# One attention-and-mixture network of four layers on one core: weights split inside the first pass, loads by need, a new order of steps

## The chip, the cores and the metric

The kernel runs on one core of a Trainium2 chip. The metric is the device time of one execution in microseconds (us). TensorE (PE) multiplies, VectorE (DVE), ScalarE (ACT) and GpSimd (POOL) do the rest, and SyncE (SP) issues all DMA transfers from its own in-order queue. Each engine runs its instructions in order and waits on semaphores for the others. SBUF is the on-chip memory of 128 partitions, PSUM the accumulator memory that PE writes.

## The reference, cut

The batch has 16 elements of 256 tokens x 256 features. Each element goes through four layers, and each layer is an attention over a context and a feed-forward part, both added with a tanh gate:

```python
x = x + tanh(g_xattn[0]) * L0_xattn(layernorm(x), ctx)   # 32 half heads of 8, differential attention
x = x + tanh(g_ffn[0])   * L0_ffn(layernorm(x))          # three cycles of a gated coupling net
x = x + tanh(g_xattn[1]) * L1_xattn(ctx, layernorm(x))   # 8 heads of 64, 512 keys, masked
x = x + tanh(g_ffn[1])   * L1_ffn(layernorm(x))          # mixture: 2 shared + 8 routed experts, silu
x = x + tanh(g_xattn[2]) * L2_xattn(layernorm(x), ctx)   # 16 heads of 16
x = x + tanh(g_ffn[2])   * L2_ffn(layernorm(x))          # inner attention, then 8 experts, gelu, top 2
x = x + tanh(g_xattn[3]) * L3_xattn(layernorm(x), ctx)   # one head
x = x + tanh(g_ffn[3])   * L3_ffn(layernorm(x))          # relu, rounded to 8-bit floats
```

L2_ffn is the second mixture. For each of its eight experts it needs `h1 = gelu(m @ w1 + b1)` and `h1 @ w2`, with w1 of 256 x 512 and w2 of 512 x 256.

## The kernel before

**Passes and steps.** Two batch elements are worked on at a time (slots 0 and 1); eight passes make up the batch. The work of one element is cut into named steps with a number: l0.max.0.3 is the fourth row maximum of layer 0 for element 0. One list, SCHEDULE, holds all 4288 steps; the string ORDER writes out by hand, one character per step, from which of 18 lists the next step comes (9 lists for each slot: the main chain, four for context work, one for values and back transposes, one for the mean path of f0, one for init, one for the first steps of layer 0). Every engine walks the same SCHEDULE and issues its own part of each step. So the order of work on PE, ACT, DVE and POOL is this one order, and steps of pass 1 stand mixed among the last steps of pass 0.

**Names.** ctxT, l0.ln, l0.xT, l0.k, l0.v, l0.ks, l0.q, l0.qs, l0.max, l0.shift, l0.exp, l0.pv, l0.out make up the first attention. l0.max is PE (L561) and one DVE reduction of 128 x 1024 (L1146). l0.shift turns the maxima (DVE L1160 to L1165, PE L502). f0.h1, f0.h2 (L512), f0.h3 (L713) and f0.t (L717) are the chain of the coupling net, each of which needs the activation that ACT makes of the one before. f2.up (PE L765) and f2.down (PE L775) are the second mixture: up is followed by a gelu on ACT (L884) and by a cast and a subtraction on DVE (L1458, L1459), down by an addition to x on DVE (L1116). PSUM has three work banks for all these products: the n-th product waits until the one three before it was read.

**The split weights.** The second mixture multiplies in the fast reduced-precision form of fp32, three products for one: each weight w is kept as hi (w rounded) and lo (w - hi). Before the schedule starts, eight experts are split: SP loads the raw expert into va (L1556), ACT copies it rounded into ksp (L870), DVE subtracts into qsp (L1349), and SP stores both to the DRAM tensor split (L1554, L1555), two experts in flight. ACT then waits until all stores are done before its first step of the schedule. In each of the eight passes SP loads hi and lo of each expert back from split, into va_hi and stream_lo, a ring of two experts.

**The launch.** SP loads all resident weights in one transfer (L1540), then stage (selection matrices, L1541), then context (cx) and x of both slots (L1546, L1547). DVE waits for the resident weights and does a chain of small setup operations (L1301 to L1342), among them four casts of the selection matrices (L1330); ACT does tanh and exp for it (L862, L864). PE waits for s_setup 1 (after the cast of w2q, L1332). ksp lies in the upper half of k1; l0.ks writes it, and l0.max and l0.exp read it.

Of the kernel before, what the change touches and what calls it, by code (L numbers as in the profile page):

```python
# [10 lines left out]
P = 128  # L11
# [34 lines left out]
    ("ident", 128), ("g_x", 4), ("g_f", 4), ("lam", 32), ("subln", 16),  # L46
# [14 lines left out]
RESIDENT_COLS = sum(n for _, n in RESIDENT)  # L61
LATE_COLS = sum(n for _, n in LATE)
# [6 lines left out]
class HeadPlan:  # L69
# [122 lines left out]
LISTS = 9  # L192
# [4 lines left out]
def lists_of(s):  # L197

    def aside(step):
        if step[0] in FIRST:  # L200
            return len(ASIDE)
        kinds = [n for n, whats in enumerate(ASIDE) if step[0].split(".")[-1] in whats and step[0] != "l3.pv"]
        return kinds[0] if kinds else None

    main, context = slot_steps(s), context_steps(s)
    every = context[0] + main
    return [[x for x in steps if aside(x) is None] for steps in (main, *context)] \
        + [[x for x in every if aside(x) == n] for n in range(len(ASIDE) + 1)]
# [3 lines left out]
    "A718A18HG111A8H8AH88A8H88HHH888888HH8H8888888HHH0H0HHH50505H50HH0HHH50509559055E0E59E99EE99E0E9095E509EE9E500E9E95950E95"  # L212
    "E2590EEE09029090696076G09F06009B90F0F009F09B0920B0000929B099000990009900009000909090095905095995950959095099099595795909"
    "E090E93E9EEE909E0900EE0E099G030900C9C90990990990390909090990099009909309809900900C90C00090000090909905905909509595090959"
    "055995990E9E09E9E9E90E907EE00E09009080G90009000099999009990990059095095095099550095595H9E90E9E009E4900E9E974EE01E091GD91"
    "9D9A91098990988089809A890980808988098090898A0909A89089080897800HH90G0H90H0H9088091090HH0909HH000H99550A05050H5H0H50H50H5"
    "H055095H05H0H5050H9H9550H9959E95E709E9E9E9E9E9E09E0E9E90E9E29E0E99E6E6E60690020909090090F09F09BF0F90909009B90900229909B9"
    "00090G090900000B0990095095590959909059590595990995959090E9EE99E3E79E9E9EE00E39000933900C90909900909090090099099099099G09"
    "9009009C0900990C90C00909000900990090905509990509950590505957959890E9E90E9E9E9E09E0E00E00090G9090000900090099990909905905"
    "09590599050590595949597940E9E09E900E09E9E190E8EH0E19H91G919890D89D9A98A89808A909A0890908H890980H98098088089H80H98909078H"  # L220
    "09H010H90900G90H8080H9A0H90009980009H95500505H050505H905H095505H0H505H050H50H9H55H9959E9E9E9E90E92E9E0E9E09E9E9E09E9E9E9"
    "0E6EE606690020099900090F0F09F09F90B9B07090990009992G90B0020900900900090090B50909959095995059999059909550959599E090E9EE9E"
    "90E9E97EE0E090090093003909099C99G09909900990099090900390909903099C9090C09C9900990000000090099009550990509590505095595990"
    "E9E90EE99E9E900EE0E07090G09090000900900009999090H099505909509509509959095549579890E9E90E0E908E909E94E0E1E019D9191G998098"
    "D9A0898A9A890A89H0890898098H08H909809800H9098H0980H90HH900899000908808987001908H090H9HH00950H0H5H0H55900G5050H5H5500H59H"
    "09H505HA09550099505E9592E59E9E90E9E9E9EE9E0E909E9E9E9E90E0E6E60G966002090900900900990FF79FF900B0090909B0999B902002009000"
    "900900990090505909959959B09095995995990059595907E0E99EE90E09E9E9EE0E003909039303G090999090090909009909C0909090990990099C"
    "090909C90000909000C00009099509905909590590995050595959890E9E09E9E9E9E90E070EE009000900900900009G999900999089090950959059"
    "095905050955995E90E9E07H9E0904EE0994EE0GD1E019D9911998A09889089A80A89HA8908H89980H890890H89H0909808H9H098H09HH09H08H0900"
    "909078G0A098080910908090H9H00905H50H05095050H5050H59H0550H505050H5909H50595995E97E9E9E09E9E9E09E0E9E9E09E9E9E069E960E2E6"  # L230
    "0E600090B0009009B009090F0G9F09F0029B9BF902900090909090920909009909900505050995905995905599999099959599E90E097E9E09EEE993"
    "EE0GE00093093090C90999009900990099009909090099009903099C90090C9090C009090009009900990990505909509505905059595980E990E90E"
    "9E97E9H0E9E00E0E0G0909090009000009099890990095905909590590950950995549959E09E9E90HE0907E09E94EE10E0G9D19D11999809899A089"
    "08909098089980889080898098908980890890A870900AAH909H0H1H9HHH090HGH0H990H0A998009088000H50H5H0590505H05H050H5055H0505H050"
    "955H090H595995E097E9E9E92E9E9E09E0E9E9E9E90E9E096E960EBE6EG609200029990009009FF9F00F909090B090990990290B9000900009000090"
    "900509505959900599955900559597909999B9099E90E9E0E990EEE990EEE0930933093C0090099900990909099099090900990090G909C90H9900C9"
    "090C009900090090900990990550909590590505909559H59E09E900E9E9E9E79E00E0E0900G90090009090000099990909950909590590959059095"
    "0595959E089E0E0990E940E7E9948E0E1D0E1G9D991A9910989088980A8980889A8A98090H98089089H80H9089H0H98H090898H0909H0090098090GH"
    "088097A01H090909H00905H050H5H0H505095050H590H55H5H909H500H5099505905E95E925E9E9E9E9E90E9EE0E9009E9E9E9E90EE6E60006290609"
    "990700900F9F09F0B9F909009009B90909209B020090090000090G9B900059990559090595950995090999959595990E90E09EE9E9E0E909EEGE0093"  # L240
    "090C907039099909900990099009900909090003309C0099099099C990C0090000000909099050995095095990590950599557990E9EH090E9E9E9E0"
    "9E00E0000E00900990090000G999H909909950095059095099509590955495909E9E9800E9E7908E09E49E0E10E190199GD19D9A809899089A890A89"
    "8A908H9H0H809089H90H980H0898H09H908908089009G0A9089090H07899H8019089900088000H50HH50505H05H05H5005H05505H95009H595H0950H"
    "0995E5E959E9E9E9E9E9E009EE9E0E990E9E90E69E2606E6E00920029900909F0090GF0F909F90B0B90970990299009B00B090000009009909900595"
    "00595050590959059995995999099099E9E9EE907E90E09E090EE0E09090C093099990099099099G00909309090909099003399C090CC90909000009"
    "9000000909905099590950950950959509595909E09E9E09E9E0900E79E00E00E00900909009G09009999090990590959095909509509505957959E9"
    "0E9E90E9E090E09EEE09094G9990D9990990909090090909099090490900900D900909090990099900909909"
# [10 lines left out]
SCHEDULE = in_order()  # L258

# [24 lines left out]
def build(nc, x_in, ctx_in, mask_in, resident_in, stage_in, moe1_in, moe2_in, out):  # L284
    with ExitStack() as ctx:
# [75 lines left out]
        k1, ksp, pt_spread = [], [], []  # L361
# [38 lines left out]

        s_res = sem("s_res")
        s_raw = [sem("s_raw0"), sem("s_raw1")]
        s_split_hi = sem("s_split_hi")
        s_split_lo = sem("s_split_lo")
        s_kept = [sem("s_kept0"), sem("s_kept1")]
# [55 lines left out]
        def split_buffers(e):  # L461

            i = e % 2
            return (va[i][:, 0:MOE2_COLS], ksp[i][:, :, :].rearrange("p a t -> p (a t)"), qsp[i][:, :, :].rearrange("p a t -> p (a t)"))
# [14 lines left out]
        def pass_of(s):  # L479

            return s // SLOTS
# [3 lines left out]
        def _(pe):  # L485
# [40 lines left out]
            def spread_attention(plan, what, s, u):  # L526
# [12 lines left out]
                elif what in ("ks", "qs"):  # L539

                    w = take(st + "." + what, s, u)
                    pe.wait_ge(*after("s_lo", st + "." + what[0], s))
                    sel = {32: {"q": sel8q, "k": sel8k}, 64: {"q": sel16q, "k": sel16k}}[plan.rows][what[0]]
# [191 lines left out]
            def ffn_2(what, s, e):  # L735
# [20 lines left out]
                elif what == "up":  # L756

                    pe.wait_ge(S[f"s_moe2_{e % RING2}"], 32 * (pass_of(s) * MOE2 // RING2 + e // RING2 + 1))
# [100 lines left out]
        def _(act):  # L859
            act.wait_ge(s_res, 16)  # L860
            for j, (name, a) in enumerate((("g_x", 0), ("g_f", 4))):
# [879 lines left out]
```

## Time and profile before

| | |
|---|---|
| median of 3 runs | 5006.4 us (5000.1 to 5006.8) |
| profiled execution | 5007.3 us |
| its span, first to last instruction | 5005.5 us |
| PE busy | 4456.6 us, 89% |
| DVE busy | 2957.9 us, 59% |
| ACT busy | 1929.4 us, 39% |
| mean granted TensorE clock | 0.948 of full |
| HBM read / written | 219.1 / 21.0 MB |

The span is one profiled execution. "Idle before" is time in which an engine waited for the instruction named behind the arrow. A window row gives each engine's busy time in one stretch. PEclk 1.00 is the 2.4 GHz level of TensorE's clock, 0.50 the 1.2 GHz level, and values between are means over a stretch.

### The profile page before, as it was taken

What the parts mean: (1) busy time and instruction counts of PE and PEld (TensorE: products, weight loads), DVE (VectorE), ACT (ScalarE), POOL (GpSimd) and SP (SyncE); (2) the same over time, 40 slices, a digit from 0 to 9 for tenths busy, and PEclk for the clock granted to TensorE, in tenths of its full rate; (3) what the DMA queues carried; (4) which work ended last, traced back from release to release, by engine and by line L of the source; (5) the groups of instructions that cost most, each with busy time, mean ns of one, the idle gap of its engine ahead of it and who ended that gap; (6) DMA issues with size and microseconds to landing.
All of it is one profiled execution on the core that took longest, in us unless ns stands there. A gap on an engine that the chain in (4) does not pass through costs nothing.

```text
span 5005.5 us, 74404 instructions
## 1 busy us (share of the span) xinstructions
PE 4456.6 (89%) x29184; PEld 3371.1 (67%) x29184; DVE 2957.9 (59%) x7749; ACT 1929.4 (39%) x3134; POOL 109.2 (2%) x196
## 2 busy tenths in 40 slices
PE   2798898989989899898998989989899988989889
PEld 1467685766756677576775758667596675856658
DVE  4556666566655566556666465655665556655555
ACT  2332535434353342433434343442434425343242
POOL 0000000000000000000000000000000000000000
PEclk9899999999989999999999989999899999999999
DMA  7001020011200111001210003001030010200012
GB/s 289 1 13 36 26 110 26 13 36 60 77 26 16 34 77 60 26 16 33 85 68 9 30 20 127 35 1 49 18 118 26 13 36 26 110 26 13 28 38 102
DMA packets 53785, 244.88 MB, mean 49 GB/s; under 512 B 5056, under 2 KB 21440, under 8 KB 31680
## 3 DMA queue, kind: packets, MB, share of 16 engines
q1 hardware_dynamic: 53440, 240.11, 13.0%
q8 instruction: 237, 3.88, 0.3%
q14 instruction: 108, 0.88, 0.1%
HBM read 219.12 MB, written 20.97 MB: 48 GB/s over the span
## 4 chain that ended last, share of the span: by engine, by line
PE 61%; DVE 9%; ACT 3%; issue 2%; POOL 0%; DVEq 0%; ACTq 0%
PE w L512 13%; PE w L522 8%; PE o L657 7%; PE w L765 7%; PE w L775 6%; PE w L502 3%; PE o L650 3%; PE w L578 3%; DVE mx L1146 2%; PE w L628 2%; PE w L613 2%; PE w L561 2%; PE w L669 1%; PE w L631 1%; DVE x L1116 1%
## 5 line engine op out<-in xcount | busy, mean ns | idle before, releaser
L1146 DVE TENSOR_REDUCE mx<-w 128x4 f32<-128x1024 f32 x512 | 606.8, 1221 | 154.9 <-PE w L561 128.2
L933 ACT ACTIVATE pt_spread<-w 128x1024 f32<-128x1024 f32 x512 | 518.8, 1024 | 294.6 <-PE w L578 277.9
L657 PE MATMUL o<-pt_spread,va 128*32 128x256 f32 x4096 | 533.8, 395 | 18.9 <-ACT pt_spread L933 17.5
L884 ACT ACTIVATE oth<-w,res 128x256 f32<-128x256 f32 x656 | 277.3, 471 | 614.1 <-PE w L765 435.1
L512 PE MATMUL w<-xnT,stream 128*128 128x256 f32 x1792 | 421.8, 385 | 8.0 <-DVE tmp L1110 3.8
L512 PEld LDWEIGHTS w<-xnT,stream 128*128 128x128 f32 x1792 | 340.4, 192 | 58.8 <-DVE tmp L1110 4.4
L765 PE MATMUL w<-qodd,va_hi 128*128 128x256 f32 x2048 | 350.1, 285 | 5.6 <-DVE x L1116 4.3
L657 PEld LDWEIGHTS o<-pt_spread,va 128*32 128x32 f32 x4096 | 203.6, 111 | 192.8 <-issue 48.2
L1116 DVE SCALAR_TENSOR_TENSOR x<-w,gate,x 128x256 f32<-128x256 f32 x512 | 224.2, 479 | 174.3 <-PE w L775 143.6
L561 PE MATMUL w<-ksp,qsp 32*128 32x256 f32 (+1 forms) x2048 | 255.5, 362 | 58.6 <-DVE mx L1146 30.4
L765 PEld LDWEIGHTS w<-qodd,va_hi 128*128 128x128 f32 x2048 | 285.7, 189 | 17.0 <-DVE x L1116 7.7
L561 PEld LDWEIGHTS w<-ksp,qsp 32*128 32x128 f32 (+1 forms) x2048 | 164.6, 217 | 153.1 <-DVE mx L1146 60.9
L578 PEld LDWEIGHTS w<-qsp,ksp 32*128 32x128 f32 (+1 forms) x2048 | 148.0, 189 | 173.8 <-issue 129.3
L578 PE MATMUL w<-qsp,ksp 32*128 32x256 f32 (+1 forms) x2048 | 241.0, 331 | 20.1 <-DVE qsp L1165 13.3
L876 ACT ACTIVATE oth<-o 128x256 f32<-128x256 f32 (+1 forms) x384 | 146.8, 382 | 265.8 <-PE o L650 159.3
L512 PE MATMUL w<-xnT,res 128*128 128x256 f32 x768 | 226.1, 442 | 22.5 <-ACT xnT L876 14.8
L650 PE MATMUL o<-pt,va 128*65 128x256 f32 x1024 | 238.1, 379 | 0.1
L1410 DVE TENSOR_REDUCE mx<-w 128x2 f32<-128x1024 f32 x128 | 154.1, 1226 | 114.0 <-PE w L615 113.9
L522 PE MATMUL w<-stream,oth 128*128 128x256 f32 x640 | 173.8, 396 | 37.3 <-DVE oth L1427 33.6
L765 PE MATMUL w<-qodd,stream_lo 128*128 128x256 f32 x1024 | 205.2, 282 | 0.0
L933 ACT ACTIVATE pt<-w 128x1024 f32<-128x1024 f32 x128 | 131.1, 1024 | 188.3 <-PE w L631 188.2
L512 PEld LDWEIGHTS w<-xnT,res 128*128 128x128 f32 x768 | 160.9, 220 | 61.7 <-issue 27.8
(269 smaller groups left out, 8222.2 us busy)
## 6 DMA issues: line engine op xcount, KB each, us to landing
stream_lo<-split SPq DMA_DIRECT2D x64, 1024.0 KB, 4.8
va_hi<-split SPq DMA_DIRECT2D x64, 1024.0 KB, 6.9
stream<-in_moe_dram SPq DMA_DIRECT2D x80, 384.0 KB, 3.1
stream<-in_resident_dram SPq DMA_DIRECT2D x8, 2048.0 KB, 7.4
va<-in_moe_dram SPq DMA_DIRECT2D x8, 1024.0 KB, 10.4
split<-ksp SPq DMA_DIRECT2D x8, 1024.0 KB, 5.6
split<-qsp SPq DMA_DIRECT2D x8, 1024.0 KB, 7.9
stream<-in_resident_dram SPq DMA_DIRECT2D x8, 1024.0 KB, 4.7
```

Of the source, the lines that this page charges most:

```text
L512: mm = pe.matmul(w[:, col0 + j * T:col0 + j * T + T], weight[:, k, (m0 + j) * P:(m0 + j + 1) * P], act[:, k, :], start=(k == 0), stop=(k = ...
L522: mm = pe.matmul(w[:, o:o + n], act[:, k, tt * P:(tt + 1) * P], weight[:, k, :], start=(k == 0), stop=(k == kc - 1))
L561: mm = pe.matmul(w[:, a * 512 + tt * T:a * 512 + (tt + 1) * T], qsp[s][b:b + plan.rows, c, tt * P:(tt + 1) * P], ksp[s][b:b + plan.rows, c ...
L578: mm = pe.matmul(w[:, a * 512 + kt * T:a * 512 + (kt + 1) * T], ksp[s][b:b + plan.rows, c, kt * P:(kt + 1) * P], qsp[s][b:b + plan.rows, c ...
L650: mm = pe.matmul(o[0:L1_DIM + 1, 0:T], by_heads1(s)[:, kt, u, :], p[:, kt * T:(kt + 1) * T], start=(kt == 0), stop=(kt == KT - 1))
L657: mm = pe.matmul(o[g:g + 32, 0:T], by_heads(plan, s)[:, kt, plan.v_of(h), :], p[:, a * 512 + kt * T:a * 512 + (kt + 1) * T], start=(kt == ...
L765: mm = pe.matmul(w[:, j * T:(j + 1) * T], wt[:, k, j * P:(j + 1) * P], a[:, k, :], start=(n == 0), stop=(n == len(parts) - 1))
L775: mm = pe.matmul(w[:, tt * D:(tt + 1) * D], a[:, k, tt * P:(tt + 1) * P], wt[:, k, :], start=(n == 0), stop=(n == len(parts) - 1))
L884: h = act.activation(dst[:, c, :], w[:, c * T:(c + 1) * T], func, bias=bias[:, c:c + 1], **more)
L933: act.activation(exp_buffer(plan.name + ".exp", s, u), w[:, :], ACT.Exp, scale=scale).then_inc(S["s_P"], 1)
L1116: h = dve.scalar_tensor_tensor(x[s][:, tt, :], w[:, tt * stride:tt * stride + D], gate_ap(tt), x[s][:, tt, :], ALU.mult, ALU.add)
L1146: dve.tensor_reduce(mx[s][:, :, 2 * u:2 * u + 2].rearrange("p t a -> p a t"), w[:, :].rearrange("p (a t k) -> p a t k", a=2, t=TT), AX_X, ...
```

## The change

- The loop that splits the weights ahead of the schedule is gone. Eight steps f2.split take its place in SCHEDULE, in a tenth list of slot 0, all in pass 0. In each, ACT writes hi straight into va_hi and DVE writes lo straight into stream_lo, where up and down read them. raw is a new name for the place of ksp.
- In pass 0 SP loads raw experts in place of hi and lo, and stores hi and lo to split for the passes after. PE's up waits for s_wlo in pass 0. l0.ks of pass 1 waits for split 6 or 7, l0.init of pass 1 and SP's load of f3_w1 for the stores.
- The resident load is cut in two. The first 2178 columns (of 10171) hold what the first steps need, ones8 and ones16 among them; stage is cut into selections (1024 columns) and the rest. SP issues first slice, selections, context and x, rest of resident, rest of stage.
- Engines wait for the rest, and DVE and ACT do the setup, where the first step comes that is not in EARLY. In the new order that is l0.shift.0.0, the 43rd step, behind 21 steps l0.max.
- ORDER is a new string of 4296 steps. All steps of before are in it, in other places.

```diff
-    ("ident", 128), ("g_x", 4), ("g_f", 4), ("lam", 32), ("subln", 16),
+    ("ident", 128), ("ones8", 1), ("ones16", 1), ("g_x", 4), ("g_f", 4), ("lam", 32), ("subln", 16),
...
+FIRST_COLS = 4 * 512 + 128 + 2
+SELECT_COLS = 4 * 256
...
-LISTS = 9
+LISTS = 10
...
+        + [[("f2.split", s, e) for e in range(MOE2)] if s == 0 else []]
...
+EARLY = ("ctxT", "l0.k", "l0.v", "l0.ks", "l0.ln", "l0.xT", "l0.q", "l0.qs", "l0.max", "l0.init", "l1.cln")
+FIRST_LATE = next(x for x in SCHEDULE if x[0] not in EARLY)
...
+            raw.append(nc.alloc_sbuf_tensor_at(f"raw{s}", [P, MOE2_COLS], F32, offset=nc.sbuf_base - half))
...
-            pe.wait_ge(s_res, 16)
-            pe.wait_ge(s_setup, 1)
+            pe.wait_ge(s_first, 16)
             for step, s, u in SCHEDULE:
+                if (step, s, u) == FIRST_LATE:
+                    pe.wait_ge(s_res, 16)
+                    pe.wait_ge(s_setup, 3)
...
-            for e in range(MOE2):
-                raw, hi, _ = split_buffers(e)
-                act.wait_ge(s_raw[e % 2], 16 * (e // 2 + 1))
-                if e >= 2:
-                    act.wait_ge(s_kept[e % 2], 32 * (e // 2))
-                act.activation(hi, raw, ACT.Copy).then_inc(s_split_hi, 1)
...
+                    if plan is L0 and pass_of(s) == 1:
+                        act.wait_ge(*after("s_wlo", "f2.split", 0, MOE2 - 2 + s % SLOTS))
...
+                elif step == "f2.split":
+                    if u < 2:
+                        act.wait_ge(*after("s_pv", "f2.pv", u, F2.units - 1))
+                    else:
+                        for other in range(SLOTS):
+                            full(act, "f2.down", other, u - RING2)
+                        act.wait_ge(s_kept[u % 2], 32 * (u // 2))
+                    act.wait_ge(s_raw[u % 2], 16 * (u // 2 + 1))
+                    act.activation(expert2(u)[0], raw2(u), ACT.Copy).then_inc(S["s_whi"], 1)
...
+                elif step == "f2.split":
+                    dve.wait_ge(*after("s_whi", step, s, u))
+                    if u < RING2:
+                        for other in range(SLOTS):
+                            full(dve, "f1.down", other, MOE1 - 1)
+                    hi, lo = expert2(u)
+                    dve.tensor_tensor(lo, raw2(u), hi.bitcast(F32), ALU.subtract).then_inc(S["s_wlo"], 1)
...
-            sp.dma_start(res[:, :], resident_in[:, 0:RESIDENT_COLS]).then_inc(s_res, 16)
-            sp.dma_start(stream[:, :], stage_in).then_inc(s_stage, 16)
+            sp.dma_start(res[:, 0:FIRST_COLS], resident_in[:, 0:FIRST_COLS]).then_inc(s_first, 16)
+            sp.dma_start(stream[:, 0:SELECT_COLS], stage_in[:, 0:SELECT_COLS]).then_inc(s_sel, 16)
...
+            sp.dma_start(res[:, FIRST_COLS:], resident_in[:, FIRST_COLS:RESIDENT_COLS]).then_inc(s_res, 16)
+            sp.dma_start(stream[:, SELECT_COLS:], stage_in[:, SELECT_COLS:]).then_inc(s_stage, 16)
...
+                if p == 0:
+
+                    for e in range(RING2):
+                        full(sp, "f2.exp", both[e], F2.units - 1)
+                        sp.dma_start(raw2(e), moe2_in[e]).then_inc(s_raw[e % 2], 16)
+                    for e in range(MOE2):
+                        hi, lo = expert2(e)
+                        sp.wait_ge(*after("s_wlo", "f2.split", 0, e))
+                        if e + RING2 < MOE2:
+                            sp.dma_start(raw2(e + RING2), moe2_in[e + RING2]).then_inc(s_raw[e % 2], 16)
+                        sp.dma_start(split[e, 0], hi.bitcast(F32)).then_inc(s_kept[e % 2], 16)
+                        sp.dma_start(split[e, 1], lo.bitcast(F32)).then_inc(s_kept[e % 2], 16)
```

## Rows read from the trace of the kernel before

**Rows 1.** The page, busy time and share of the span of each engine.
```profile
PE 4456.6 (89%) x29184; PEld 3371.1 (67%) x29184; DVE 2957.9 (59%) x7749; ACT 1929.4 (39%) x3134; POOL 109.2 (2%) x196
```
**Rows 2.** Timeline: start, duration, engine, line, operation, count, idle before and releaser.
```profile
15.36 0.30 ACT L862 ACTIVATE tg<-res 128x4 f32<-128x4 f32 x2 [13.35 <-DMA res<-in_resident_dram]
15.42 0.17 DVE L1301 MEMSET onesf<- 128x128 f32 x1 [15.42 <-DMA res<-in_resident_dram]
...
24.39 1.94 PE L502 MATMUL w<-res,cx 128*128 128x128 f32 x8 [24.39 <-DVE w2q L1332]
...
25.99 0.15 DVE L1342 TENSOR_SCALAR nlam<-nlam 128x1 f32<-128x1 f32 x1
...
89.92 1.08 ACT L876 ACTIVATE ctxT<-w 128x512 f32<-128x512 f32 x2 [8.69 <-DMA split<-qsp]
...
90.58 5.48 PE L512 MATMUL w<-ctxT,res 128*128 128x256 f32 x16 [64.24 <-ACT ctxT L876]
...
135.88 0.20 DVE L1160 CAST hib<-mx 128x64 bf16<-128x64 f32 x1
```
**Rows 3.** Windows at the start: busy of each engine, PEclk, DMA share, GB/s.
```profile
24.36:83.47 59.11, 1.94 (x8) 1.57 (x8) 19.57 (x13) 15.37 (x9) 0.00 (x0) 1.00 0.93 375
...
109.90:135.90 26.00, 16.40 (x104) 10.91 (x104) 24.06 (x22) 2.64 (x3) 0.00 (x0) 0.59 0.00 1
```
**Rows 4.** Groups by line, 25 to 84 us: busy, mean ns, idle before.
```profile
L1349 DVE TENSOR_TENSOR qsp<-va,ksp 128x2048 fp32r<-128x2048 f32 x8 | 18.3, 2292 | 39.1 <-ACT ksp L870 39.1
L870 ACT ACTIVATE ksp<-va 128x2048 fp32r<-128x2048 f32 x8 | 15.3, 1908 | 40.4 <-DMA va<-in_moe_dram 40.4
```
**Rows 5.** Groups by line on DVE, 109 to 136 us.
```profile
L1146 DVE TENSOR_REDUCE mx<-w 128x4 f32<-128x1024 f32 x21 | 24.0, 1218 | 2.8 <-PE w L561 2.8
```
**Rows 6.** Windows between the ends of the second mixture, longest, shortest and sum.
```profile
1934.00:2551.00 617.00, 561.98 (x3668) 424.07 (x3668) 371.19 (x966) 238.45 (x390) 13.34 (x25) 0.94 0.12 43
...
4359.00:4958.00 599.00, 539.30 (x3471) 408.04 (x3470) 339.76 (x915) 226.13 (x374) 13.48 (x24) 0.94 0.12 43
sum 4234.00, PE 3867.27 PEld 2925.43 DVE 2534.92 ACT 1663.85 POOL 94.72; mean PE 552.47 PEld 417.92 DVE 362.13 ACT 237.69 POOL 13.53
```
**Rows 7.** Windows of the launch's first 10 us; the last number is GB/s.
```profile
0.00:5.00 5.00, 0.00 (x0) 0.00 (x0) 0.00 (x0) 1.28 (x1) 0.20 (x4) 1.00 0.77 260
5.00:10.00 5.00, 0.00 (x0) 0.00 (x0) 0.00 (x0) 0.00 (x0) 0.00 (x0) 1.00 0.92 399
```
**Rows 8.** DMA issues, 0 to 120 us: KB each, median us from issue to landing.
```profile
res<-in_resident_dram SPq DMA_DIRECT2D x1, 5085.5 KB, 14.6
stream<-in_stage_dram SPq DMA_DIRECT2D x1, 2048.0 KB, 19.0
```
**Rows 9.** Windows: pass 0's second mixture, the stretch after it, the last pass's mixture.
```profile
620.00:722.00 102.00, 100.28 (x833) 94.91 (x832) 68.62 (x123) 30.99 (x67) 0.69 (x2) 1.00 0.36 135
724.00:758.00 34.00, 31.10 (x191) 25.18 (x189) 21.59 (x61) 11.81 (x22) 0.67 (x2) 1.00 0.00 1
4870.00:4958.00 88.00, 87.89 (x731) 87.25 (x729) 49.59 (x106) 23.52 (x57) 0.00 (x0) 1.00 0.41 156
```
**Rows 10.** Groups by line on DVE, 4870 to 4960 us.
```profile
L1459 DVE TENSOR_TENSOR oth_lo<-oth,ob_hi 128x512 fp32r<-128x512 f32 x29 | 20.1, 693 | 1.0
L1116 DVE SCALAR_TENSOR_TENSOR x<-w,gate,x 128x256 f32<-128x256 f32 x32 | 14.0, 479 | 20.9 <-PE w L775 20.9
L1458 DVE CAST ob_hi<-oth 128x512 fp32r<-128x512 f32 x29 | 12.4, 427 | 16.5 <-ACT oth L884 16.5
```
**Rows 11.** Groups by line on PE, whole span: h2, h3 and t of f0.
```profile
L512 PE MATMUL w<-oth,res 128*128 128x256 f32 x192 | 57.0, 423 | 24.5 <-ACT oth L884 23.0 <-ACT gsm L971 1.5
L713 PE MATMUL w<-oth,res 128*64 128x256 f32 x96 | 32.6, 425 | 15.8 <-ACT oth L884 15.8
...
L717 PE MATMUL w<-res,oth 64*128 64x1 f32 x192 | 31.0, 263 | 14.3 <-ACT oth L986 13.9
```

More of the change, by code:

```diff
@@ L248 @@
+    "A57AA5FAF0AFA0F0AF0AF0AFFF0A0AAAA0AHAA0AA0A04A0A0A0A0EA0A00A0A4A0A00A00EA0A00A0A0AA0A0A0A0A0AA0A"
 )
@@ L360, in build @@
         qsp, qz = shared("qsp", [P, 8, T], F32R, "qz", [P, L1_HEADS, T])
-        k1, ksp, pt_spread = [], [], []
+        k1, ksp, pt_spread, raw = [], [], [], []
         for s in range(SLOTS):
@@ L459, in expert2, with raw2 @@
             return va_hi[e % RING2][:, :], stream_lo[:, cols]
-        def split_buffers(e):
-            i = e % 2
-            return (va[i][:, 0:MOE2_COLS], ksp[i][:, :, :].rearrange("p a t -> p (a t)"), qsp[i][:, :, :].rearrange("p a t -> p (a t)"))
+        def raw2(e):
+            return raw[e % 2][:, :]
         def first_and_second(w):
@@ L859, in _ @@
         def _(act):
-            act.wait_ge(s_res, 16)
-            for j, (name, a) in enumerate((("g_x", 0), ("g_f", 4))):
-                act.activation(tg[:, a:a + 4], W_[name], ACT.Tanh).then_inc(s_setup_act, 1)
-            act.wait_ge(s_setup, 2)
-            act.activation(nlam[:, 2:4], nlam[:, 0:2], ACT.Exp).then_inc(s_setup_act, 1)
-            for e in range(MOE2):
-                raw, hi, _ = split_buffers(e)
-                act.wait_ge(s_raw[e % 2], 16 * (e // 2 + 1))
-                if e >= 2:
-                    act.wait_ge(s_kept[e % 2], 32 * (e // 2))
-                act.activation(hi, raw, ACT.Copy).then_inc(s_split_hi, 1)
-            for n in range(2):
-                act.wait_ge(s_kept[n], 32 * (MOE2 // 2))
-            act.wait_ge(s_setup, 3)
+            act.wait_ge(s_first, 16)
             def evac(out_ap, in_ap, sig):
@@ L946, in _ @@
                 stage, what = step.split(".") if "." in step else (step, "")
+                if (step, s, u) == FIRST_LATE:
+                    act.wait_ge(s_res, 16)
+                    for j, (name, a) in enumerate((("g_x", 0), ("g_f", 4))):
+                        act.activation(tg[:, a:a + 4], W_[name], ACT.Tanh).then_inc(s_setup_act, 1)
+                    act.wait_ge(s_setup, 2)
+                    act.activation(nlam[:, 2:4], nlam[:, 0:2], ACT.Exp).then_inc(s_setup_act, 1)
+                    act.wait_ge(s_setup, 3)
                 if step == "ctxT":
@@ L1314, in once @@
                 dve.wait_ge(setup_chain, count[0])
-            lam = W_["lam"].rearrange("p (n d) -> p n d", n=4)
-            for j in range(2):
-                once(dve.tensor_tensor(tmp[:, 8 * j:8 * j + 8], lam[:, 2 * j, :], lam[:, 2 * j + 1, :], ALU.mult))
-                once(dve.tensor_reduce(nlam[:, j:j + 1], tmp[:, 8 * j:8 * j + 8], AX_X, ALU.add))
-            once(dve.memset(first_row[0:1, :], 1.0))
-            once(dve.tensor_scalar(subw[:, :], W_["subln"], 1.0 - LAMBDA_INIT, None, ALU.mult))
@@ L1338, in _ @@
-            dve.wait_ge(s_setup, 2)
-            dve.wait_ge(s_setup_act, 3)
-            once(dve.tensor_tensor(nlam[:, 0:1], nlam[:, 3:4], nlam[:, 2:3], ALU.subtract))
-            dve.tensor_scalar(nlam[:, 0:1], nlam[:, 0:1], LAMBDA_INIT, None, ALU.subtract).then_inc(s_setup, 1)
-            dve.wait_ge(s_setup, 3)
-            for e in range(MOE2):
-                raw, hi, lo = split_buffers(e)
-                dve.wait_ge(s_split_hi, e + 1)
-                if e >= 2:
-                    dve.wait_ge(s_kept[e % 2], 32 * (e // 2))
-                dve.tensor_tensor(lo, raw, hi.bitcast(F32), ALU.subtract).then_inc(s_split_lo, 1)
+                h = dve.tensor_copy(t[:, :, :], sg[:, 256 * j:256 * j + 256].rearrange("p (a b) -> p a b", a=2))
@@ L1596, in _ @@
                     context_and_first(p + 1)
-                for e in range(MOE2):
+                if p == 0:
[9 more added lines that the diff above has]
+                        sp.dma_start(split[e, 1], lo.bitcast(F32)).then_inc(s_kept[e % 2], 16)
+                    for n in range(2):
+                        sp.wait_ge(s_kept[n], 32 * (MOE2 // 2))
+                for e in range(MOE2 if p else 0):
                     n = e % RING2
```

166 lines of the change are left out of this document (86 added, 80 removed), and 4 rows, old and new, of tables (RESIDENT, SIGNALS).

## The prediction

> **What bounds the kernel now.** I read the busy shares first: PE works 89% of the span, DVE 59%, ACT 39% [rows 1]. TensorE bounds the kernel, but only as a mean over stages with different limits, so I cut the span into stretches.
>
> The first stretch is not bound by PE at all. Until 15.4 us everything waits for one load of all resident weights; VectorE then works through its setup, and PE starts its first transposes at 24.39 us [rows 2]. After those eight transposes PE does nothing until 90.58 us [rows 2]. The window 24.36 to 83.47 us shows why: PE 1.94 us busy, DVE 19.57, ACT 15.37, DMA engines 93% busy [rows 3]. It is the split of the second mixture's weights, a loop over eight experts with two buffers. Its own arithmetic is 8 x 2.292 us on DVE and 8 x 1.908 us on ACT [rows 4], and the rest of the time it waits for 24 MB to pass through the DMA queue. The scheduled steps of ACT may not begin before it is over: the first ctxT eviction stands at 89.92 us [rows 2].
>
> Then comes a stretch that DVE bounds: from 109.90 to 135.90 us DVE is 24.06 us busy of 26 [rows 3], 21 reductions of 1.218 us [rows 5], and the first shift's DVE work begins at 135.88 us [rows 2]. From there on eight passes follow. I cut them where the last second-mixture matmul of each pass ends: seven intervals, 4234 us together, mean 604.9, shortest 599, longest 617, PE 552 us busy in each on average [rows 6]. Each interval has its own hand-searched order of the same work, so their spread tells what an order is worth.
>
> **The launch.** The order that the diff gives has the same 21 reductions ahead of the first shift as before, and the same number of steps ahead of the first reduction, so I move this whole piece along as a block, hung on the start of l0.k on PE (90.58 us before).
>
> When can it start? The first slice is 2178 columns, 1.12 MB; the selections 0.52 MB; each context or x tile 0.26 MB. The first step, ctxT of slot 1, needs the slice and cx1, which stands 2.43 MB into the queue. The queue moved 260 GB/s in its first 5 us and 399 GB/s in the next 5 [rows 7], so 1.30 MB by 5 us and 2.43 MB by 7.8 us. The resident load of before (5.21 MB) would have moved by 14.35 us on this reckoning and released ACT about 1 us later [rows 2, 7]; with that, cx1 is there at 8.8 us. Half of the eight transposes (1.94 us for all [rows 2]) takes 1 us, the eviction 0.54 us (1.08 for two) and the hops 0.2, so l0.k starts at about 10.6 us: **80.0 us earlier**. The selections (four casts of 0.29 us) and the first layernorm are on DVE before PE asks for them at about 16 us, and cost nothing; without that cover they would cost their own 1.2 us.
>
> This needs the transfers to be served in the order of issue. The 5 MB load landed 14.6 us after its issue although 2 MB of stage were queued 0.5 us behind it, and that one landed after 19.0 us [rows 8]: one after the other. Had all queued loads shared the engines evenly, the first slice would be there only when about 4.9 MB have moved, some 5 us later. I keep 5 us as the far bound. The Trainium skill ("DMA: Bandwidth & Descriptors", HWDGE ordering) says that each DMA engine consumes its descriptors in ring order, while completion is not guaranteed in that order; the rows here agree with the first half, and no row shows the second. By that rule the sum stays as above; by even sharing it would be 5 us worse.
>
> **The setup that is put off.** It isn't gone: DVE does it at the first shift, in its own queue, and PE waits there for s_setup 3. Before, DVE's chain ran from 15.42 to 26.14 us (the last two small operations start at 25.80 and end at 26.14) [rows 2], 10.7 us. The four selections with their gaps, 1.3 us, go ahead; nlam, tanh and exp stay in. Left: 9.4 us. DVE is busy 24 of 26 us in front of this place [rows 3], so nothing hides it; behind it are the shift's DVE work, then the slot-1 reductions, and PE and ACT wait for them. By then (55 us) the resident and stage loads have landed (8.4 MB at some 400 GB/s, 22 us). Bounds: 7.4 us (DVE's 2 idle us absorb something) and 13 us (table load and hops between ACT and DVE come on top). I take 9.4. **Launch in all: 80.0 - 9.4 = 70.6 us gained**, bounds 62 and 73. TensorE's clock stood at half in this DVE-bound stretch (mean 0.59 [rows 3]), and will again; it costs little there since DVE sets the pace. The load of the first cross-attention weights moves behind setup 1, to about 62 us, and is needed after 140: free. SP's loads of x behind it too.
>
> **The split inside pass 0.** It adds eight ACT copies of 1.908 and eight DVE subtractions of 2.292 us, 15.3 and 18.3 us, and exchanges the sixteen 1 MB loads of this pass for eight loads and sixteen stores. In pass 0 the mixture is PE's: 100.28 of 102 us, DVE 68.62, ACT 30.99 [rows 9]. In the last pass, which has no next pass mixed in, the mixture takes 88 us, 11 us for one expert of both slots, with DVE 49.59 us [rows 9]; its parts for one expert and both slots are 4 x (0.427 + 0.693) + 4 x 0.479 = 6.4 us [rows 10]. With the split DVE has 8.7 of 11 us and ACT 4.8. It fits, but no reductions fit beside it. The new order says so itself: before, 16 reductions of pass 1 stood inside pass 0's mixture, now 8, all behind the last split, because ksp is the raw buffer and l0.ks must wait for splits 6 and 7. The other 8 (9.8 us of DVE) move behind the mixture, chiefly to 724 to 758 us, where DVE has 12.4 us idle and PE 2.9 [rows 9]. They fit just so. ACT now waits in its queue for PE to finish down(e-2), with the next gelu behind it; up of e+2 comes one up and one down of both slots later, 11 us, against 4.2 us for a split. SP holds nothing behind its wait for the stores but f3_w1, needed 30 us later.
>
> PE has next to nothing to win here, 1.7 us of idle time, so a gain is excluded beyond 2 us. The other end is every split open on the chain: 8 x (1.908 + 2.292) = 33.6 us. I take **+4 us**, nearer the low end, because the mixture's row has PE busy 98% and the 3 us of PE idle after it may at most double.
>
> **The order.** All else in it is moved about. As random redraws of orders as good as these (spread of one interval about 7 us), seven intervals and the two ends move the sum by 20 us either way. A count leans slightly to the new one. In the gated feed-forward f0 a step that directly follows its producer on PE makes PE wait: h2, h3 and t have 54.6 us of PE idle between them [rows 11] for 59 such neighbours, 0.93 us each. The new order has 49. That is -9 us; l3.max has 7 neighbours in place of 3 and f1.down 7 in place of 5, which gives some 4 back. I take **-5 us**, bounds -27 and +20.
>
> **Sum.** Profiled execution 5007.3 us (span 5005.5 and 1.8 around it), 0.9 above the median of 5006.4. 5007.3 - 70.6 + 4 - 5 = 4935.7; against the median 4935.
>
> **Rivals.**
> - The split is exposed. ACT's and DVE's waits are in order, and every split delays the gelu and the hi/lo step behind it. Price 33.6 us instead of 4, 4965; with the store and load of each expert on the chain as well, the cadence of the old loop, 59 us / 8 = 7.4 us an expert, gives 59 in all and 4990. Against: 11 us of PE work cover each. Chance 0.12 for 4958 to 4990.
> - A better order. All intervals like the shortest, 7 x 5.9 = 41 us less than their mean: 4899. Against: the old order was found for the same costs. Chance 0.10 for under 4912.
> - **Slower.** The new order is a bad one in the steady passes: every interval like the longest, 7 x (617 - 604.9) = 85 us: 5025, slower by 0.4%. Without the 5 us that I credit the sum is 4940, so it turns to slower once the intervals are 9.5 us longer on average than before, and to slower by 0.2% from 10.9 us. Against: one of seven shows 617. Chance 0.02; 0.02 more for a sum that lands within 0.2%.
> - The change does not do what it says: the loads share the queue after all, and the first step starts only when all 8.4 MB have landed, at 22 us. Then l0.k starts at 24 us, 66.4 earlier, less 9.4 for the setup: 57 us in place of 70.6, 4948. Against: [rows 8]. Chance 0.04, and inside the range.
>
> **How the numbers follow.** The forecast, 4935, has 0.70; its own range is 4912 to 4958. The range over all cases is 4908 to 4964: it leaves out half of the better order and most of the exposed split. 0.2%, 10 us, is about what can be told from no change. Faster 0.96, same 0.02, slower 0.02.
>
> **What would show it.** Right: first PE work near 9 us, l0.k near 11, a hole of 9 to 10 us on PE at about 55 us with DVE in its setup; the end of pass 0's mixture near 724 - 70 + 2 = 656 us with PE over 95% busy in it; intervals of about 604. Wrong: PE idle before L765 in pass 0 ended by the split's subtraction, reductions that push l0.exp of pass 1 behind f3.out, or intervals whose mean leaves 600 to 609.

## The result

| | median | runs | profiled span | clock |
|---|---|---|---|---|
| before | 5006.2 us | 5000.1 to 5006.8 | 5005.5 us | 0.948 |
| after | 4894.4 us | 4893.8 to 4896.2 | 4894.4 us | 0.953 |

The ratio is 0.978, 95% interval 0.9763 to 0.9797. The change takes off 112 us, where I had forecast 71 and at most 98. The direction is right, the size is not: 4894 lies below the range's 4908.

The launch first. Timeline of the kernel after (start, duration, engine, line, operation, idle before and releaser):

```profile
10.05 1.94 PE L508 MATMUL w<-res,cx 128*128 128x128 f32 x8 [10.05 <-DMA cx<-in_ctx_dram]
...
11.22 1.28 ACT L875 ACT_TABLE_LOAD   x1 [11.22 <-PE w L508]
...
13.16 5.45 PE L518 MATMUL w<-ctxT,res 128*128 128x256 f32 x16 [1.18 <-ACT ctxT L875]
...
30.92 23.85 DVE L1163 TENSOR_REDUCE mx<-w 128x4 f32<-128x1024 f32 x21 [1.99 <-PE w L568]
...
54.75 0.17 DVE L1335 MEMSET onesf<- 128x128 f32 x1
...
64.13 0.19 DVE L1177 CAST hib<-mx 128x64 bf16<-128x64 f32 x1
...
65.03 3.33 PE L508 MATMUL w<-res,mp 128*128 128x128 f32 x16 [8.68 <-DVE mp L1179]
```

The first shift's DVE work starts at 64.13 in place of 135.88 us [rows 2]: 71.8 us, forecast 70.6. The put-off setup is the stretch from 54.75 to 64.13 us, 9.4 us as forecast, and PE sees it as 8.68 us of idle time in front of its transposes.

The rest of the kernel, from the first shift to the end, before and then after (length, busy of PE, PEld, DVE, ACT, POOL with counts, PEclk, DMA share, GB/s):

```profile
138.80:5005.50 4866.70, 4420.53 (x28964) 3344.19 (x28962) 2895.56 (x7646) 1898.55 (x3104) 107.72 (x188) 0.95 0.12 43
```

```profile
66.70:4894.40 4827.70, 4390.70 (x28974) 3327.37 (x28972) 2918.94 (x7654) 1917.67 (x3115) 110.48 (x188) 0.96 0.13 45
```

Here lie the other 39 us, although 23 us of DVE work and 19 us of ACT work have come in. Take PE busy from the length: PE is idle 446.2 us before and 437.0 after, 9 us less. The other 30 us are **PE busy time**: practically the same matmuls take 4390.7 in place of 4420.5 us. That is the clock. The trace's clock records put TensorE at its 1.2 GHz level for 522 us of the span before and 461 us after; behind the first shift it is 498 and 424 us. Over the twelve kernels below that have no filler, PE busy behind the first shift follows the time at 1.2 GHz there: 0.41 us of busy for each us, from 4378 us at 392 (e6) to 4421 us at 498 (before), and none lies more than 6 us off that line.

Intervals between the ends of the second mixture, of after, as [rows 6] of before:

```profile
1851.40:2465.80 614.40, 552.09 (x3654) 417.74 (x3654) 365.71 (x966) 238.74 (x390) 13.98 (x24) 0.96 0.12 43
...
4259.50:4846.80 587.30, 532.46 (x3465) 405.78 (x3464) 337.90 (x912) 226.18 (x374) 13.98 (x24) 0.95 0.12 43
...
sum 4211.00, PE 3843.21 PEld 2910.93 DVE 2549.37 ACT 1666.75 POOL 97.13; mean PE 549.03 PEld 415.85 DVE 364.20 ACT 238.11 POOL 13.88
```

Seven intervals take 4211 in place of 4234 us; the other 16 us fell in pass 0, between its first shift and the end of its mixture. The second mixture of pass 0, with the splits inside, and the stretch behind it (compare [rows 9]):

```profile
530.00:634.00 104.00, 101.57 (x846) 97.73 (x844) 77.23 (x145) 45.42 (x78) 0.68 (x2) 1.00 0.54 199
636.00:678.00 42.00, 36.86 (x215) 27.89 (x213) 29.61 (x69) 11.73 (x21) 0.61 (x2) 0.96 0.00 1
```

PE stays 98% busy with the splits running beside it. Behind the mixture, in the 42 us up to the first exps of pass 1, PE is idle for 5.1 us, against 2.9 in the 34 us before.

### The profile page after: what moved, and what is told of

Same layout as the page of the kernel before. It is cut to its first block, busy times and chain, and to the rows that moved or that the text cites. A ratio compares the mean times of both kernels' runs of the same rounds, so it can differ in the third digit from the quotient of the medians.

```text
span 4894.4 us, 74395 instructions
## 1 busy us (share of the span) xinstructions
PE 4428.5 (90%) x29184; PEld 3355.0 (69%) x29184; DVE 2962.4 (61%) x7749; ACT 1932.6 (39%) x3136; POOL 111.9 (2%) x196
## 4 chain that ended last, share of the span: by engine, by line
PE 77%; DVE 15%; ACT 5%; issue 3%; POOL 0%; DMA 0%; DVEq 0%; SPq 0%; ACTq 0%
PE w L518 17%; PE w L528 10%; PE o L664 9%; PE w L775 8%; PE w L785 7%; PE w L508 4%; DVE mx L1163 4%; PE o L657 4%; PE w L585 3%; PE w L635 3%; PE w L620 2%; PE w L568 2%; PE w L676 1%; PE w L638 1%; ACT pt_spread L934 1%
## 5 line engine op out<-in xcount | busy, mean ns | idle before, releaser
L934 ACT ACTIVATE pt_spread<-w 128x1024 f32<-128x1024 f32 x512 | 519.0, 1024 | 250.8 <-PE w L585 237.4
L1037 ACT ACTIVATE oth<-w 128x256 f32<-128x256 f32 x160 | 61.5, 384 | 356.3 <-PE w L518 356.2
```

The source lines that it names most:

```text
L934: act.activation(exp_buffer(plan.name + ".exp", s, u), w[:, :], ACT.Exp, scale=scale).then_inc(S["s_P"], 1)
```

## The experiments

All are versions of the changed kernel unless said otherwise. Medians are of 4 or 5 executions. They come from four further jobs on four chips: e1 to e4, e5 to e8, e9 and e10, e11 and e12. The changed kernel itself ran in none of them. One kernel that ran in two (e8 and e12) gave 4889.1 and 4888.6. The kernel of before scattered more: single executions from 4987 to 5012 us, medians of 4993.8, 4999.4, 5005.3 and 4999.8 us in these jobs against 5006.2 beside after. A difference against before therefore depends by up to 12 us on the job it is taken from, and one of 5 us between two kernels says little unless a row of the trace shows where it comes from.

| run | what | median us | PE idle behind the first shift | at 1.2 GHz behind it | of it near f0 |
|---|---|---|---|---|---|
| before | | 5006.2 | 446 | 498 | 130 |
| after | | 4894.4 | 437 | 424 | 72 |
| e1 | old order | 4945.3 | 456 | 486 | 117 |
| e2 | before with new order | 4960.2 | 438 | 410 | 68 |
| e3 | all loads first | 4899.4 | 436 | 420 | 75 |
| e4 | new order in pass 0 only | 4912.1 | 442 | 436 | 106 |
| e5 | splits done twice | 4928.8 | 461 | 456 | 79 |
| e6 | 1.8 us later | 4895.4 | 437 | 392 | 68 |
| e7 | old f0 stretches | 4919.9 | 451 | 453 | 109 |
| e8, e12 | setup spread | 4889.1, 4888.6 | 440, 439 | 423, 423 | 82, 75 |
| e9 | e1 with new f0 stretches | 4933.1 | 456 | 449 | 90 |
| e10 | e7 with filler | 4914.5 | 420 | 397 | 51 |
| e11 | e8 with filler | 4892.4 | 413 | 434 | 61 |

The last three columns are each from the profiled execution: lengths between the marks less PE busy, and the clock records added up; "near f0" is within three PE steps of a step of f0.

**e1, the old order.** Only ORDER differs: the old string, with the new one in the piece around the splits.

> The changed kernel with the order of before: the old order up to the end of the inner attention of pass 0, the new order only through the stretch that holds the eight splits, the old order again for the seven passes after. Launch and split as changed. Theory O, the missing 40 us come from the order: between the marks of the two traces the new order gained 16 us in pass 0 and 34 us in the passes after, so 4894 + 16 + 34 = 4944, between 4935 and 4955. Rival L, the order is worth no more than the 5 us I gave it, and launch and split gave the rest in a way I did not see: 4899, between 4893 and 4905.

4945.3, on the 4944 of theory O. Launch and split alone take the kernel from 5006 to 4945 (from 4994, by the before of this job), and the order is worth 51 us, ten times what I gave it. Launch and split gave 61 where I had 67, or 48 within this job. This kernel's launch stretch is 3.8 us longer than after's: its first shift step ends at 70.8 instead of 67.0 us, its first reduction starts at 32.65 instead of 30.92 us, and its 21 reductions have gaps that after's have not. So part of what the launch gained is the order's as well.

**e2, the new order on the kernel of before.**

> The kernel of before, its launch and its split loop untouched, with the new order (the eight split steps left out of it). Theory O: 5006 - 16 - 34 = 4956, up to 4966 since the first reductions of pass 1 stand later than this kernel needs. Rival L: 4996 to 5006. The half-clock time, 524 us in the trace of before, should fall to about 450 by O.

4960.2, inside theory O's span, and the half-clock time fell to 437 us for the whole span (forecast 450). So the order is worth something on the old kernel too, without any split or launch: 46 us against the 5006.2 of the first job, 34 against the before of its own job. 5 us of it lie ahead of the first shift, whose step starts on PE at 131.7 in place of 136.8 us. This kernel also prices the split, since the order is the same as after's. Pass 0 and pass 1 of e2, which has no split in them, and then of after:

```profile
133.50:701.30 567.80, 509.30 (x3391) 385.68 (x3390) 330.81 (x873) 223.73 (x361) 12.98 (x22) 0.95 0.11 41
701.30:1312.10 610.80, 561.92 (x3710) 424.02 (x3709) 379.10 (x975) 243.88 (x394) 13.61 (x24) 0.95 0.12 43
```

```profile
67.00:635.80 568.80, 511.32 (x3390) 387.12 (x3389) 348.47 (x881) 238.20 (x369) 13.36 (x22) 0.95 0.16 58
...
635.80:1246.70 610.90, 561.97 (x3711) 423.88 (x3709) 379.04 (x975) 244.16 (x394) 14.00 (x24) 0.95 0.12 43
```

568.8 against 567.8 us, and 610.9 against 610.8: with 17.6 us more of DVE work and 14.5 more of ACT work in pass 0, the split costs 1 us in the new order. The pair with the old order, before and e1, differs by more: 585.2 against 592.2 us for pass 0, and 4.7 us by the end. But e1 has the new order around its splits, so this pair doesn't price the split alone.

**e3, all loads first.**

```diff
-FIRST_LATE = next(x for x in SCHEDULE if x[0] not in EARLY)
+FIRST_LATE = SCHEDULE[0]
...
-            context_and_first(0)
             sp.dma_start(res[:, FIRST_COLS:], resident_in[:, FIRST_COLS:RESIDENT_COLS]).then_inc(s_res, 16)
             sp.dma_start(stream[:, SELECT_COLS:], stage_in[:, SELECT_COLS:]).then_inc(s_stage, 16)
+            context_and_first(0)
```

> The changed kernel, but all launch loads are issued first and the whole setup is done ahead of the first step, as before; the split stays in pass 0. It prices the loads by need alone. My reckoning: PE starts at 26.2 in place of 10.05 us, l0.k at 28.2 in place of 13.2, 15 us later, but the 9.8 us hole before the first shift is gone: + 5 us, 4900. Rival: the hole costs nothing where it stands (PE would wait there anyway), then the whole 15 us show: 4909.

4899.4, forecast 4900. PE starts 17 us later than in after:

```profile
26.91 1.94 PE L508 MATMUL w<-res,cx 128*128 128x128 f32 x8 [26.91 <-DVE nlam L1364]
```

but it has no hole ahead of the first shift, whose step starts at 71.6 in place of 65.0 us. Loading by need is worth 5 us of the 72 on the median and 6.6 by these rows: the rest of the launch gain is the split loop that is gone and, by e1, some 4 us of order. Most of what the early start wins, the setup takes back at a place where DVE is the bound.

**e4, the new order in pass 0 only.**

> The changed kernel with the new order only through pass 0 up to the first shift of pass 1, and the old order for everything after. Theory O with the gain spread over the passes as the marks show (16 us in pass 0, 34 later): 4894 + 34 = 4928, between 4922 and 4936. Rival: most of the order's gain sits in pass 0, where the split had to be fitted in, and the rest is its echo: 4894 to 4905.

4912.1, between the two theories and in neither span. Against after it costs 18 us for seven old-order passes, against e1 it gains 33 us, while 23 us of difference are in launch and pass 0 as such. The missing 10 are the balance of intervals with the very same steps in both kernels: from inside pass 0's mixture to the end their lists agree. The last two intervals of e1:

```profile
3691.40:4296.10 604.70, 553.50 (x3636) 418.48 (x3636) 361.97 (x962) 242.18 (x392) 13.77 (x24) 0.96 0.12 44
4296.10:4894.60 598.50, 539.04 (x3468) 407.92 (x3468) 339.29 (x913) 226.33 (x374) 13.87 (x24) 0.94 0.12 43
```

and of e4:

```profile
3675.90:4273.50 597.60, 545.66 (x3637) 413.75 (x3636) 362.00 (x962) 241.79 (x392) 13.74 (x24) 0.97 0.13 44
4273.50:4861.90 588.40, 528.00 (x3468) 400.66 (x3468) 339.23 (x913) 226.02 (x374) 13.83 (x24) 0.96 0.12 43
```

Same instructions, the same DVE and ACT time within 0.4 us, PE idle 51 to 52 and 59 to 60 us in both. But PE is busy 7.8 and 11.0 us less in e4, and the intervals are 7.1 and 10.1 us shorter. The clock records have 51 and 75 us at 1.2 GHz in e1 and 31 and 48 in e4. So one order can fall into different clock patterns, and a microsecond at half clock costs 0.35 to 0.4 us. Behind pass 0 the two kernels have 399 and 369 us at 1.2 GHz, and e1 takes 9.7 us longer there.

**e5, the splits done twice.** The ACT copy and the DVE subtraction of each split are each issued a second time.

> The changed kernel with each of the eight splits done twice over on ACT and on DVE (another 15.3 and 18.3 us of work in pass 0, the same result). If the split costs by DVE's and ACT's time (DVE then has 11 of 11 us per expert in pass 0): + 10 to 20 us, all of it as PE idle in pass 0: 4904 to 4914. Rival, the one split cost only by displacing reductions behind the mixture and its own work is hidden: + 0 to 5 us, 4894 to 4900.

4928.8, 34 us more, beyond both theories. Pass 0 of e5, to compare with the 568.8 us of after:

```profile
67.10:670.60 603.50, 523.98 (x3391) 399.79 (x3390) 366.06 (x890) 252.99 (x377) 13.35 (x22) 0.93 0.16 55
```

PE idle rises by 22 us (79.5 against 57.5), and PE busy by 12.7 us, as the clock falls too. The first split is nearly free and the second one costs more than its own DVE time. The expectation had DVE full, 11 of 11 us. The trace shows something else. Here are one of the stalls in the mixture and the window from 530 to 634 us, in which after has PE busy for 101.57 us and DVE for 77.23:

```profile
569.19 2.29 DVE L1477 TENSOR_TENSOR stream_lo<-raw,va_hi 128x2048 fp32r<-128x2048 f32 x1
...
571.59 0.77 PE L776 MATMUL w<-qodd,va_hi 128*128 128x256 f32 x2 [3.68 <-issue]
...
530.00:634.00 104.00, 85.42 (x620) 83.66 (x620) 68.53 (x109) 42.68 (x67) 0.00 (x0) 0.89 0.48 172
```

DVE is less busy than in after, not full. Four times PE starts the next up 0.1 us after the second subtraction has ended (at 571.6, 592.1, 609.8 and 627.2 us), having stood idle for 2.9 to 3.7 us. What ran out is the time between the release of an expert's buffers and its up: copy, copy, subtraction, subtraction take 8.4 us one after the other, where a single split takes 4.2. That is the exposed chain of the first rival, and each stall is paid a second time through the clock, 0.89 of full in this window and 1.00 in after's.

**e6, everything 1.8 us later.**

```diff
+                once(dve.memset(mp[:, :, :], 0.0))
                 dve.memset(mp[:, :, :], 0.0)
```

> The changed kernel with one memset of mp more (1.8 us) in DVE's setup ahead of the first shift. Nothing else moves: every step after it is the same and in the same order. Theory C, the half-clock stretches depend on when PE's quiet moments come and not only on the order: PE's idle time after the first shift stays within 2 us, but the half-clock time moves by 10 us or more, and the time differs from 4896 (4894 + 1.8) by up to 8 us either way. Rival, the clock follows the order alone: 4896 within 2 us and the same half-clock stretches, shifted.

The median is 4895.4, which is the rival's time. In the profiled execution the span is 4884.6 us, 9.8 less than after's with 2 us more to do; PE idle behind the first shift is 437 us in both, the time at 1.2 GHz 392 against 424. The other three executions took 4894.6 to 4896.6 us. So the pattern differs from one execution of a kernel to the next, by about 10 us. The rival's other half, the same half-clock stretches, fails in that execution. But that it was the shift of 1.8 us that moved them, as theory C says, is not shown, since three of four executions kept after's time.

**e7, the old order in f0 only.** The relative order of the steps between the first l0.out and the second l1.q of each pass is the old one; all else is new.

> The changed kernel with the old relative order in each pass between the first l0.out and the second l1.q (the stretch of the coupling net f0), the new order elsewhere. Theory F, the order's gain in the steady passes lies in f0, where half-clock time fell from about 125 us in the two old-order traces to 70: it comes back, half-clock + 40 us, time + 16 to 22 us: 4910 to 4916. Rival, the gain is spread and f0 takes only its eighth part: 4896 to 4900.

4919.9, 25 us more than after, a bit over theory F's span: f0 and its surroundings hold half of the order's 51 us. It costs 14 us of PE idle and 29 us at 1.2 GHz. How such a stretch looks, in the pass with the greatest difference, before and then after:

```profile
4457.00:4582.00 125.00, 109.16 (x524) 74.71 (x523) 76.37 (x256) 50.34 (x85) 4.36 (x6) 0.88 0.00 1
```

```profile
4359.00:4466.00 107.00, 93.42 (x465) 63.14 (x464) 71.05 (x236) 47.28 (x80) 3.36 (x4) 0.95 0.00 1
```

PE idle is 15.8 and 13.6 us, nearly the same. The stretch is 18 us shorter, and at 0.95 of the clock instead of 0.88; but it also has 59 fewer matmuls in it, which stand elsewhere, so the 18 us are not all gain.

**e8, the setup spread.** DVE's memsets go to the very start, where DVE waits for the first load; only the two lambda products stay ahead of the first shift; the rest stands ahead of the first l0.back, while PE has exps and values to do. PE, ACT and POOL wait for it at the first l0.norm.

```diff
+SECOND_LATE = next(x for x in SCHEDULE if x[0] not in EARLY + ("l0.shift", "l0.exp", "l0.pv", "l0.back"))
...
                 if (step, s, u) == FIRST_LATE:
-                    rest_of_setup()
+                    first_of_setup()
+                if (step, s, u) == ("l0.back", 0, 0):
+                    rest_of_setup()
```

> The changed kernel with DVE's memsets of the setup at the very start (they need no load), the two lambda products and nothing else ahead of the first shift, and the rest of the setup ahead of l0.back, where PE has exps and values to do; PE and POOL wait for it only at the first l0.norm. It takes away 9 of the 9.8 us that DVE spends ahead of the first shift. If that hole was exposed, as forecast: 4894 - 9 = 4885, give or take 5 for the clock. Rival, the rest costs as much where it is put now: 4892 to 4896.

4889.1, and 4888.6 in e12: 5 us less than after, inside the span but at its short end. The step of the first shift ends at 58.4 in place of 67.0 us, 8.6 us earlier; 6 us of it were given back by the end of pass 0 (575.2 us from there, in place of 568.8), 2.2 of them as idle time and most of the others as 13 us more at 1.2 GHz, and the later intervals returned some of that. By the median this is the fastest kernel of all; the 5 us alone are within what a kernel's own executions differ by, and what carries the gain is the first shift's place.

**e9, the mirror of e7.** The kernel of e1 with the new f0 stretches.

> The mirror of e7: the kernel of e1 (old order, splits in pass 0) with the new relative order only in each pass's stretch from the first l0.out to the second l1.q. Theory F: 4945 - 25 = 4920, between 4914 and 4928; half-clock time near f0 falls from 117 us to about 75. Rival, the new f0 stretches are good only behind the new order's first attention: 4938 to 4946.

4933.1, a gain of 12 us, half of what theory F wanted and more than its rival. The eight f0 stretches, read from the end of the first l0.out to the end of the second l1.xT, are 26 us shorter together (862 against 888 us), but they also have 81 fewer matmuls in them; read up to the start of the second l1.q they differ by 3 us (900 against 903), with 71 matmuls more. What is free of this count is PE's idle time in them, 116 against 124 us, and the time at 1.2 GHz, 90 against 117: 8 us and, at 0.4 us each, another 11. The f0 part is real; that not all of it arrives in the total shows that it is not independent of what stands around it.

**e10 and e11, filler.** Four small matmuls for nothing, wherever h2, h3 or t directly follows its producer on PE.

```diff
+                if ("f0." + what, s, c) in NEIGHBOURS:
+                    filler(4)
...
+                for _ in range(n):
+                    pe.matmul(obank[0][:, 256:512], sel1[:, 0, :], sel1[:, 0:2, :].rearrange("p a b -> p (a b)"), start=True, stop=True)
```

> The kernel of e7 (old f0 stretches) with work for nothing: at the 59 places where f0.h2, h3 or t directly follows its producer on PE, four bf16 matmuls of 128x256 into an unused half of a PSUM bank, ahead of the wait. They use PE for about 0.4 us in gaps of 0.9 us. Theory C, the half clock follows PE's quiet moments: the half-clock time near f0 falls from 109 us to 80 or less, and the time by 8 to 15 us, to 4905 to 4912, though PE has more to do. Rival, the clock does not care, or the gaps were not open long enough: half-clock time within 10 us of e7's and 4918 to 4930.

PE has 236 matmuls more to do, and the kernel is 5 us faster than e7, 4914.5, which is outside both spans: 8 to 15 us were wanted. Its profiled execution is the fastest of its four (4899.4, the others 4913.2 to 4916.4), and in it the time at 1.2 GHz near f0 is 51 us instead of 109. How much of that fall the other three executions had is not known. That a filler cuts the half-clock time near f0 is likely, since e11 shows a fall too, but 5 us of median don't show a gain in time.

> The kernel of e8 (setup spread, new order throughout) with the filler of e10 at its 49 neighbours in f0. If idle time and half clock near f0 shrink as in e10, where the median fell 5 us for 59 places: 4889 - 4 = 4885, between 4879 and 4889. Rival, with the new order's f0 the gaps are so small that the filler costs what it takes: 4889 to 4896.

4892.4 against 4888.6 of e12 beside it, both with runs from 4882 up: no gain. PE idle behind the first shift fell by 26 us and the time at 1.2 GHz near f0 from 75 to 61, but all in all the kernel stood at half clock for 10 us more, and the fillers use PE themselves: PE busy is 30 us more.

> The kernel of e8 once more, beside e11 on the same chip, for the comparison of the two: 4889, between 4885 and 4892.

4888.6, as forecast.

## Why the prediction was wrong

**The launch** came out right, 71.8 us for 70.6, in part by luck. l0.k started at 13.16 us, 77.4 us earlier, where I had 80.0: PE started at 10.05 where I had 8.8, and a table load of 1.28 us, which had been hidden in the wait of before, stood ahead of the first eviction; I had left it out. My start also leaned on the resident load having moved by 14.35 us, which needs 438 GB/s behind the first 10 us; at the 399 of [rows 7] it is 14.8, which makes my start 8.4, not 8.8. The setup cost 9.4 us, as said. What made up for the late start is that the piece did not move along as a block: the first reduction came 17.8 us behind l0.k's start in place of 19.3, and the 21 reductions took 23.8 us in place of 26.0. With the old order (e1) both lengths are as before, so these 4 us are the order's. The launch alone gave 68. The loads were served in the order of issue, and the rival of shared loads is out. DMA issues of after, KB each and us from issue to landing: the slice was there after 5.0 us with 7.2 MB queued behind it.

```profile
res<-in_resident_dram SPq DMA_DIRECT2D x1, 3996.5 KB, 16.2
...
res<-in_resident_dram SPq DMA_DIRECT2D x1, 1089.0 KB, 5.0
```

**The split** was right in kind and small either way: +4 forecast, +1 by e2 beside after, in profiled spans. The exposed rival is out for this kernel. But the doubled split shows that DVE's budget (8.7 of 11 us) was not the thing to count: it stalls PE through the length of the chain from the copy to the last subtraction, with DVE a third idle (68.5 of 104 us busy).

**The step that failed is "The order".** I wrote -5 us with bounds of -27 and +20; e1 against after gives -51, e2 against before -46 (-34 in its own job).

- The term had only half of the mechanism. I priced PE's idle time at f0's neighbours, -9 us and some given back. h2, h3 and t wait 49.9 us after (22.7, 15.1 and 12.1; 54.6 before [rows 11]), so these waits gave 4.7 of the 9, and PE idle behind the first shift fell by 9 us in all. The clock I put at nothing. A quiet moment can be paid twice, once as waiting and once as half clock over the matmuls around it: e7 has 14 us more idle and 29 us more at 1.2 GHz than after, e5 24 and 31. The two don't always go together; e1 has 9 us more idle than before and 12 us less at half clock. From before to after the half-clock time behind the first shift fell by 74 us, which at 0.4 us each is 30 us: the whole fall of PE's busy time.
- The bound was drawn from the spread of seven intervals, as if the new order were a random draw of the same kind. The profile had the other number in view: the mean clock of 0.948, that is about 520 us at 1.2 GHz in the span, worth some 200 us (estimate, at 0.4 us each) if it could all be had back. A search over orders can reach into that, so the bound on the gain's side was far too near.
- The rival of a better order was there, with 0.10 and 4899 us. The time is almost the measured one; the mechanism, all intervals as short as the shortest, is not. They still spread from 587 to 614 us, and two fifths of the gain behind the launch came in pass 0.
- My own sign would not have caught it. I called the forecast wrong if the intervals' mean left 600 to 609 us; it is 601.6, inside, though the seven intervals gained 23 us. The sign that did speak was pass 0's mixture, which ended at 635.8 us where I had 656.

The two gains that I could price from rows, launch and split, add to 66.6 us forecast; e1 measured 61 for them on the median. The miss of 41 us is 46 us of order that I did not see, less 6 us that launch and split fell short.

**What stays open.** Where the old orders of before, e1, e4 and e7 have 106 to 130 us at 1.2 GHz near f0, the new ones of after, e2, e3, e5, e6, e8 and e12 have 68 to 82, and e9, new in f0 alone, has 90: this part belongs to the order. Elsewhere the half-clock time wanders by 30 us between kernels with equal steps (e1 and e4 behind pass 0), or between after and one execution of e6, whose steps are the same. How much of the 51 us is such a pattern I can't settle. From e1 to after the profiled spans differ by 48 us: 4 in the launch, 23 in pass 0 and 21 behind it, and of those last 21 e4 has 10 with e1's own steps. So some 10 us behind pass 0 are not shown to be the order's, and single executions of one kernel differ by 10 us (e6) up to 25 (before). What is in the new order's other half, outside f0, was not tried.

## What to carry to other kernels

Where PE sets the pace, take its idle time and its half-clock time as two separate accounts, and read both for a change that reorders work: PE busy at an unchanged count of matmuls is the clock's account. A setup moved off the launch's load wait costs its full length if it lands where its own engine is the bound; look for a gap of that engine, or for memsets that need no load. Work put under a cover is free only while its chain, from the release of its buffer to its reader, is shorter than the cover, however idle its engine is: here the first 18 us of DVE work cost 1 us and the next 18, in a chain twice as long, cost 34. And a kernel's scatter is part of its result: a term of 5 us can't be tested by medians of four or five executions that differ by 10.

## What I had not expected of the hardware

- Identical instruction streams differ by 7 and 10 us an interval through the granted clock alone (e1 and e4), with PE idle equal within 1 us.
- One execution of a kernel took 10 us less than its other three, with PE idle the same and 32 us less at 1.2 GHz than after (e6).
- PE stood idle for 3.7 us at a time behind a chain of ACT and DVE work while DVE was only 66% busy (e5).
- With 236 more matmuls of no use, one execution was 15 us faster than its other three and 20 us faster than the profiled one without them (e10).
